# Narrowing a batch search, moving a small copy, and doing the last norm's row work during the gates

## The chip, the cores and the metric

The kernel runs on one core of one Trainium2 chip. The metric is device time in microseconds (us); lower is better. In the profile PE is TensorE, DVE is VectorE, ACT is ScalarE, POOL is GpSimd and SP is the engine that issues the DMAs.

## The reference, cut to what matters

There are 3327 nodes with 128 features each; `adj` is a sparse matrix with entries from 0.05 to 1 and a full diagonal. Everything is float32.

```python
# layer 0, two steps (x_a starts as x; a second branch multiplies by the row-normalized adj)
logits = (Xa @ W1.T @ W2.T) @ (Xa @ W3.T).T
probs = softmax(logits)                       # keep the largest of a row until their sum reaches 0.9
keep_sorted = cumsum(sorted) - sorted < 0.9
A = probs * mask; A = A / A.sum(-1)
Xa = A @ Xa;  Z = Z + Xf @ U1[n].T + Xa @ U2[n].T
x = layernorm(x + layernorm(X + Z) * ln_g + ln_b)
# layer 1: node_support = adj_offdiag @ x; edge_support from three attention heads with vectors a
r = sigmoid(ir + hr); z = sigmoid(iz + hz); n = tanh(inn + r * hn)
gru = (1 - z) * n + z * h                     # twice: "edge" and "node", each with its own weights
out = layernorm(x + diag[:, None] * gru_edge + diag[:, None] * gru_node)
```

## The kernel before, in words

Rows are handled as T = 26 tiles of 128, padded to 3328. The kernel is three stages one behind the other, each with one instruction stream per engine and semaphores between them: `layer0`, `normalize_and_sum` and `attention_and_gates`.

**The batch at the end of layer 0.** Of every row the largest values are found in segments (MAX8, L73) and a threshold is searched by halving an interval of float bit patterns (`solve_halving`): each halving (L222) masks and sums all candidates, compares the sum with 0.9 of the row's total (L227) and moves the middle (L229). In the second step rows whose segments don't cover their threshold are gathered into one batch of up to 128 rows; `taken_batch` searches it with segments of 16, which are 208 x 8 = 1664 candidates a row, in 16 halvings. Behind the halvings come one pass below the last middle (L235), a MAX8 over it (L240), a pass above the value found (L258) and small steps (`end`). The flags go to TensorE (`turn_flags`, L918), which turns them only after its own `late_rows`; then VectorE reads them (L1594) and selects, full width (L451, L456, L462). A flag of 256 or more, from any open row, runs `another_round` over the full width first. Meanwhile ScalarE copies the late rows' results (L1236, L1250, L1255) and GpSimd adds them (L767).

**The first norm.** In `normalize_and_sum` VectorE sums the two halves of the rows, then waits for TensorE's products of the head vectors (L1736) and copies them into V (L1866); then come the deviation (L1832), the root on ScalarE (L1797, after the squares, L1790), and in each half the rows are scaled (L1872) and added to X (L1876). X is shifted before by GpSimd, in two halves (L1725), and L1872 waits for its half. V is read by TensorE's `project`, behind the turned rows.

**The gates and the last norm.** `gates_and_output` works in 14 units: 7 chunks of 512 columns (the last has 256), each once for "edge" (g = 0) and once for "node" (g = 1). TensorE does six products a unit (`products`, L2015 to L2024) into four banks of sums, of two sets. ScalarE does the sigmoids r (L2045), z (L2049) and s (L2051). VectorE does the candidate of unit u (L2076, L2080), then the blend of unit u - 1 (L2087 to L2096). Behind all units, chunk by chunk, TensorE turns the blended columns to rows (L2034), VectorE adds them to H with their sums (L2109, L2113), ScalarE squares (L2056); then the root (L2061), the reciprocal (L2119), and VectorE norms 26 tiles (L2122). SP stores the first 13 tiles, then 12, then the last tile's 127 rows (L1995, L1999, L2002).

The order of all work is written by hand: each engine executes its stream in order.

## Time and profile before

| | us |
|---|---|
| median of 3 runs | 2689.44 (2689.21 to 2690.14) |
| the profiled execution | 2681.91 |
| its span, first to last instruction | 2680.1 |
| PE busy in the span | 2326.0 (87%) |
| DVE busy | 2159.6 (81%) |
| ACT busy | 1070.0 (40%) |
| POOL busy | 149.3 (6%) |

The rows further down are of the profiled execution; their times count from the start of its span. A row of the timeline gives the start, the duration from the first to the last instruction of a group, the engine, the line, the operation, what it writes and reads, and the number of instructions; in brackets stands the idle time before it and what ended it. The mean granted clock of TensorE is 0.95 of its full speed.

### The profile page before, as it was taken

What the parts mean: (1) busy time and instruction counts of PE and PEld (TensorE: products, weight loads), DVE (VectorE), ACT (ScalarE), POOL (GpSimd) and SP (SyncE); (2) the same over time, 40 slices, a digit from 0 to 9 for tenths busy, and PEclk for the clock granted to TensorE, in tenths of its full rate; (3) what the DMA queues carried; (4) which work ended last, traced back from release to release, by engine and by line L of the source; (5) the groups of instructions that cost most, each with busy time, mean ns of one, the idle gap of its engine ahead of it and who ended that gap; (6) DMA issues with size and microseconds to landing.
All of it is one profiled execution on the core that took longest, in us unless ns stands there. A gap on an engine that the chain in (4) does not pass through costs nothing. (4 is left out here: it accounts for less than half of the span.)

```text
span 2680.1 us, 53786 instructions
## 1 busy us (share of the span) xinstructions
PE 2326.0 (87%) x17795; PEld 1967.5 (73%) x17795; DVE 2159.6 (81%) x6687; ACT 1070.0 (40%) x1803; POOL 149.3 (6%) x342
## 2 busy tenths in 40 slices
PE   7999999878899979988976459987999999999995
PEld 2666666657677867767756459876999999999962
DVE  4777777578787888888889677757999999999956
ACT  5666666433334444334422230004344433444333
POOL 0000000111111111000010000000000000000000
PEclk8999999989999989999978769999999999999997
DMA  4000000022223322222212135542343343333320
GB/s 134 2 2 1 1 1 1 2 103 78 81 101 116 116 78 104 103 78 82 105 48 83 63 134 213 206 178 103 105 136 124 120 139 104 131 128 112 121 92 26
DMA packets 57310, 244.88 MB, mean 91 GB/s; under 512 B 6929, under 2 KB 18576, under 8 KB 43344
## 3 DMA queue, kind: packets, MB, share of 16 engines
q1 hardware_dynamic: 57040, 241.99, 25.8%
q8 instruction: 83, 1.36, 0.2%
q14 instruction: 187, 1.53, 0.2%
HBM read 235.15 MB, written 6.82 MB: 90 GB/s over the span
## 5 line engine op out<-in xcount | busy, mean ns | idle before, releaser
L2319 PE MATMUL a_acc<-H,pT 128*128 128x128 f32 x4056 | 547.8, 277 | 11.8 <-ACT a_rows L2352 3.8
L2319 PEld LDWEIGHTS a_acc<-H,pT 128*128 128x128 f32 x4056 | 495.3, 192 | 28.8 <-DVE pT L2455 20.0
L992 PE MATMUL small<-XR,wT 128*128 128x128 f32 x2756 | 379.0, 283 | 26.7 <-ACT wT L1262 26.1
L992 PEld LDWEIGHTS small<-XR,wT 128*128 128x128 f32 x2756 | 344.3, 197 | 42.6 <-ACT wT L1262 42.6
L863 PE MATMUL lg<-kT,qs 128*128 128x512 f32 (+1 forms) x742 | 339.8, 594 | 27.3 <-ACT e L1180 16.8
L73 DVE MAX8 cand<-e 128x8 f32<-128x64 f32 (+3 forms) x1898 | 302.8, 241 | 48.8 <-issue 25.3
L2455 DVE TENSOR_TENSOR pT<-a_tr,a_adjT 128x512 f32<-128x512 f32 (+1 forms) x546 | 316.7, 645 | 20.7 <-PE a_tr L2278 15.6
L2278 PE MATMUL a_tr<-ident,prob 128*128 128x128 f32 x2028 | 311.2, 273 | 10.9 <-ACTq L2346 10.9
L1262 ACT ACTIVATE wT<-tr 128x512 f32<-128x512 f32 (+1 forms) x371 | 206.7, 566 | 276.9 <-PE tr L982 275.9
L892 PE MATMUL accR<-XR,adj 128*128 128x129 f32 x2704 | 312.6, 275 | 0.0
L892 PEld LDWEIGHTS accR<-XR,adj 128*128 128x128 f32 x2704 | 308.5, 192 | 0.0
L2433 DVE CUSTOM_DVE_ANT_0 prob<-a_adj,EB 128x3328 f32<-128x3328 f32 x78 | 282.6, 3623 | 0.0
L982 PE MATMUL tr<-ident,e 128*128 128x128 f32 x1378 | 217.8, 287 | 65.6 <-DVE scalars L1516 60.0
L982 PEld LDWEIGHTS tr<-ident,e 128*128 128x128 f32 x1378 | 169.7, 148 | 117.1 <-DVE scalars L1516 62.8
L863 PEld LDWEIGHTS lg<-kT,qs 128*128 128x128 f32 x742 | 118.7, 193 | 186.5 <-ACT e L1180 142.4
L1180 ACT ACTIVATE e<-lg 128x512 f32<-128x512 f32 (+1 forms) x371 | 206.6, 566 | 107.8 <-PE lg L863 106.0
L2278 PEld LDWEIGHTS a_tr<-ident,prob 128*128 128x128 f32 x2028 | 240.9, 142 | 11.1 <-issue 11.1
L2344 ACT ACTIVATE prob<-prob,a_negmax 128x3328 f32<-128x3328 f32 x78 | 238.9, 3063 | 9.1 <-DVE a_negmax L2442 9.1
L1752 PE MATMUL g_sp<-g_adj,H 128*128 128x128 f32 x1352 | 159.2, 279 | 17.1 <-ACTq L1817 17.1
L1752 PEld LDWEIGHTS g_sp<-g_adj,H 128*128 128x128 f32 x1352 | 155.1, 194 | 18.8 <-issue 18.8
L1212 ACT ACTIVATE e<-e,scalars 128x3327 f32<-128x3327 f32 x53 | 162.0, 3059 | 8.4 <-DVE scalars L1580 8.3
L222 DVE SCALAR_TENSOR_TENSOR work<-cand,mid 128x416 f32<-128x416 f32 (+1 forms) x198 | 143.3, 758 | 10.6 <-issue 3.1
(351 smaller groups left out, 2419.8 us busy)
## 6 DMA issues: line engine op xcount, KB each, us to landing
adj<-in_adjT SPq DMA_DIRECT2D x52, 1664.0 KB, 7.2
g_adj<-in_adjT SPq DMA_DIRECT2D x26, 1664.0 KB, 6.8
a_adj<-in_adj SPq DMA_DIRECT2D x26, 1664.0 KB, 7.0
a_adjT<-in_adjT SPq DMA_DIRECT2D x156, 256.0 KB, 3.9
a_adjT<-in_adjT SPq DMA_DIRECT2D x26, 128.0 KB, 4.1
XT<-in_x_t SPq DMA_DIRECT2D x1, 1664.0 KB, 7.2
hT_scratch<-hT SPq DMA_DIRECT2D x1, 1664.0 KB, 11.3
nsT_scratch<-nsT SPq DMA_DIRECT2D x1, 1664.0 KB, 5.3
```

The costliest lines, as they stand in the source:

```text
L73: eng.max(cand[:, n, :], src[:, n * seg:min((n + 1) * seg, width)])
L863: eng.matmul(lg[bank(st, p, k, c)][:, 0:sl.stop - sl.start], qs[k][:, :], kT[:, sl], start=True, stop=True).then_inc(lg_ready, 1)
L892: mm = eng.matmul(accR[:, :], adj[k][:, j * P:(j + 1) * P], xf[:, j, :], start=False, stop=(j == T - 1))
L982: mm = eng.transpose(tr[(k * NC + c) % 2][:, o:o + P], e[b][k][:, j * P:(j + 1) * P], ident[:, :])
L992: mm = eng.matmul(accA[:, :], wT[(k * NC + c - 1) % 2][:, o:o + P], xa[:, j, 0:P], start=(j == 0), stop=(j == T - 1))
L1262: eng.activation(wT[(k * NC + c) % 2][:, 0:sl.stop - sl.start], tr[(k * NC + c) % 2][:, 0:sl.stop - sl.start], ACT.Copy).then_inc(wT_ready, 1)
L1752: mm = eng.matmul(sp[k][:, :], H[:, j, :], adj[q][:, j * P:(j + 1) * P], start=(j == 0), stop=(j == T - 1))
L2278: mm = eng.transpose(tr[g % BANKS][:, (j % 4) * P:(j % 4 + 1) * P], prob[order[n][1]][:, j * P:(j + 1) * P], ident[:, :])
L2319: mm = eng.matmul(acc[:, :], pT[g % RING][:, (j % 4) * P:(j % 4 + 1) * P], H[:, j, :], start=(j == 0), stop=(j == T - 1))
L2344: eng.activation(prob[h][:, :], prob[h][:, :], ACT.Exp, bias=negmax[h][:, :], accum_out=den[h][:, :])
L2433: eng.tensor_tensor_reduce(prob[h][:, :], adj[k][:, :], EB[:, h, :], 1.0, -3.0e38, ALU.add, ALU.max, mx[h][:, :])
L2455: eng.tensor_tensor(pT[g % RING][:, 0:width(c)], tr[g % BANKS][:, 0:width(c)], adjT[:, c * 512:c * 512 + width(c)], ALU.mult).then_inc(pT_ ...
```

## The change

It has three parts.

**Batch search.** `solve_halving` takes an argument `wide`. For the batch it is 6: after six halvings `narrow` masks the candidates that are not below the current bound, keeps the largest 8 of each 64 (26 groups, 208 values) and one more value, the largest sum so far that stayed below 0.9; the largest eighth value of a group raises `tau`, the bound above which all values are known to be among the candidates. The other ten halvings and the steps behind them run over these 209 values.

**Head vectors.** The wait for the head vectors' products and the three copies into V stand behind the second mean of the two halves.

**Gates and last norm.** Each set has three banks; z has one bank for both sets, and the turned rows have one. TensorE turns chunk c behind unit 2c + 3, VectorE adds its rows behind blend 2c + 3, at unit 2c + 4, and ScalarE squares them behind unit 2c + 5. The last two chunks come behind all units. VectorE norms 14 tiles, ScalarE 12, from a new product of mean and reciprocal; five stores instead of three.

```diff
+WIDE_HALVINGS = 6
...
         self.counts = sb("counts", [P, 2, 4])
-        self.round_cand = sb("round_cand", [P, -(-width // ROUND_SEG), 8])
+        n_round = -(-width // ROUND_SEG)
+        self.few_cand = sb("few_cand", [P, n_round * 8 + 1])
+        self.round_cand = self.few_cand[:, 0:n_round * 8].rearrange("p (a b) -> p a b", b=8)
...
-    def solve_halving(self, eng, cand, halvings):
+    def narrow(self, eng, cand, step, done):
+
+        mass, low = self.mass[:, 0:done, 0:1], self.low[:, 0:done, 0:1]
+        spare, rest = self.work[:, 0:cand.shape[1]], self.few_cand.shape[1] - 1
+        eng.tensor_tensor(low, mass, self.one("theta", 0).unsqueeze(1).to_broadcast([P, done, 1]), ALU.is_lt)
+        eng.tensor_scalar(self.round_mid[:, :], self.mid[:, 0:1], float(step), None, ALU.add)
+        eng.drain()
+        eng.scalar_tensor_tensor(spare, cand, self.round_mid[:, :].bitcast(F32), cand, ALU.is_lt, ALU.mult)
+        eng.tensor_tensor(low, mass, low, ALU.mult)
+        eng.drain()
+        segment_tops(eng, spare, cand.shape[1], self.round_cand, cand.shape[1] * 8 // rest)
+        eng.tensor_reduce(self.few_cand[:, rest:rest + 1], low.rearrange("p n k -> p k n"), AX.X, ALU.max)
+        eng.drain()
+        eng.tensor_reduce(self.one("best", 0), self.round_cand[:, :, 7], AX.X, ALU.max)
+        eng.drain()
+        eng.tensor_tensor(self.one("tau", 0), self.one("tau", 0), self.one("best", 0), ALU.max)
+        eng.drain()
+
+    def solve_halving(self, eng, cand, halvings, wide=None):
 
 
         tiles, n = range(len(cand)), len(cand)
...
         eng.drain()
         step = FIRST_STEP
         for h in range(halvings):
+            if h == wide:
+                self.narrow(eng, cand[0], step, h)
+                cand = [self.few_cand[:, :]]
+                spare = [self.work[:, 0:cand[0].shape[1]]]
             for k in tiles:
                 eng.scalar_tensor_tensor(spare[k], cand[k], self.mid[:, k:k + 1].bitcast(F32), cand[k],
                                          ALU.is_ge, ALU.mult, accum_out=self.mass[:, h, k:k + 1])
...
-                        find.solve_halving(eng, [find.fine[:, :, :].rearrange("p a b -> p (a b)")], FINE_HALVINGS)
+                        find.solve_halving(eng, [find.fine[:, :, :].rearrange("p a b -> p (a b)")], FINE_HALVINGS,
+                                           wide=WIDE_HALVINGS)
...
                     eng.tensor_reduce(total[:, half(i)], H[:, half(i), :], AX.X, ALU.add)
                     eng.drain()
                     mean(half(i))
-                eng.wait_ge(v_summed, 1)
-                for part in range(3):
-                    copy = eng.tensor_copy(V[:, part, :], vp[:, :, part % 2])
-                copy.then_inc(v_ready, 1)
                 for i in range(2):
                     deviation(0, i)
                     eng.wait_ge(x_shifted, i + 1)
...
                                                  ALU.mult, ALU.add, accum_out=total[:, t:t + 1])
                     eng.drain()
                     mean(half(i))
+                eng.wait_ge(v_summed, 1)
+                for part in range(3):
+                    copy = eng.tensor_copy(V[:, part, :], vp[:, :, part % 2])
+                copy.then_inc(v_ready, 1)
                 clear_diagonal(0, 0)
                 for i in range(2):
                     deviation(1, i)
...
     edge = sb(3, "o_edge", [P, CH])
-    sums = [banks[0:4], [banks[4], banks[7], banks[5], banks[6]]]
+    sums = [banks[0:3], banks[3:6]]
+    zp_bank, rows_bank = banks[6:8]
 
...
+    BY_VECTOR = T // 2 + 1
+    PARTS = [(0, BY_VECTOR // 2), (BY_VECTOR // 2, BY_VECTOR), (BY_VECTOR, (BY_VECTOR + T) // 2),
+             ((BY_VECTOR + T) // 2, T)]
 
     def tiles(c):
         return range(c * 4, min(c * 4 + 4, T))
 
-    def rows_bank(c):
-        return sums[c // 4][c % 4]
+    def rows_of(t):
+        return rows_bank[:, (t % 4) * P:(t % 4 + 1) * P]
 
         eng.dma_start(support[1][:, cols(NC - 1)], d["gsT"][:, cols(NC - 1)]).then_inc(chunk_loaded[NC - 1], 16)
-        eng.wait_ge(normed, 1)
-        eng.dma_start(d["out"][0:HALF * P, :].rearrange("(t p) d -> p t d", p=P), H[:, 0:HALF, :])\
-           .then_inc(stored, 16)
-        eng.wait_ge(normed, 2)
         whole = N // P
-        eng.dma_start(d["out"][HALF * P:whole * P, :].rearrange("(t p) d -> p t d", p=P), H[:, HALF:whole, :])\
-           .then_inc(stored, 16)
+        for n in (0, 2, 1, 3):
+            first, end = PARTS[n][0], min(PARTS[n][1], whole)
+            eng.wait_ge(normed[n // 2], n % 2 + 1)
+            eng.dma_start(d["out"][first * P:end * P, :].rearrange("(t p) d -> p t d", p=P), H[:, first:end, :])\
+               .then_inc(stored, 16)
         if N % P:
             eng.dma_start(d["out"][whole * P:N, :], H[0:N % P, whole, :]).then_inc(stored, 16)
-        eng.wait_ge(stored, 48 if N % P else 32)
+        eng.wait_ge(stored, 80 if N % P else 64)
 
     def products(eng):
+        def turn(c):
+            eng.wait_ge(mixed, 2 * c + 2)
+            eng.wait_ge(mean_ready, c) if c else eng.wait_ge(sup_copied, T)
+            for t in tiles(c):
+                mm = eng.transpose(rows_of(t), OT[:, t * P:(t + 1) * P], ident[:, :])
+            mm.then_inc(turned, 1)
+
         eng.wait_ge(weights, 16 * 8)
         for u in range(UNITS):
             c, g, i = u // 2, u % 2, u % 2
-            rp, zp, inp, hnp = (t[:, 0:width(c)] for t in sums[i])
+            rp, inp, hnp, zp = (t[:, 0:width(c)] for t in sums[i] + [zp_bank])
             if g == 0:
                 eng.wait_ge(chunk_loaded[c], 48)
             if u >= 2:
...
             eng.matmul(rp, Wh[g][:, 0:P], state, start=True, stop=False)
             eng.matmul(rp, Wi[g][:, 0:P], sup, start=False, stop=True).then_inc(r_summed, 1)
             eng.matmul(inp, Wi[g][:, 2 * P:3 * P], sup, start=True, stop=True).then_inc(in_summed, 1)
-            if u >= 2:
-                eng.wait_ge(z_ready, u - 1)
-            if u == 1:
-                eng.wait_ge(sup_copied, T)
+            if u >= 1:
+                eng.wait_ge(z_ready, u)
             eng.matmul(zp, Wh[g][:, P:2 * P], state, start=True, stop=False)
             eng.matmul(zp, Wi[g][:, P:2 * P], sup, start=False, stop=True).then_inc(z_summed, 1)
-        for c in range(NC):
-            if c == 0:
-                eng.wait_ge(arg_ready, UNITS - 1)
-                eng.wait_ge(z_ready, UNITS - 1)
-            if c == 4:
-                eng.wait_ge(arg_ready, UNITS)
-                eng.wait_ge(z_ready, UNITS)
-            eng.wait_ge(mixed, 2 * c + 2)
+            if u >= 3 and u % 2:
+                turn((u - 3) // 2)
+        turn(NC - 1)
+
+    def gates(eng):
+        def squares(c):
+            eng.wait_ge(mean_ready, c + 1)
             for t in tiles(c):
-                mm = eng.transpose(rows_bank(c)[:, (t % 4) * P:(t % 4 + 1) * P], OT[:, t * P:(t + 1) * P],
-                                   ident[:, :])
-            mm.then_inc(turned, 1)
-
-    def gates(eng):
+                eng.activation(sq[:, t, :], H[:, t, :], ACT.Square, bias=negmean[:, t:t + 1],
+                               accum_out=var[:, t:t + 1])
+            eng.drain()
+            eng.sem_inc(squared, 1)
+
         eng.wait_ge(biases_ready, 1)
         for u in range(UNITS):
             c, g, i = u // 2, u % 2, u % 2
             n = width(c)
-            rp, zp, inp, hnp = sums[i]
+            rp, inp, hnp = sums[i]
+            zp = zp_bank
             eng.wait_ge(r_summed, u + 1)
             eng.activation(r[i][:, 0:n], rp[:, 0:n], ACT.Sigmoid, bias=b_rz[g][:, 0:1]).then_inc(r_ready, 1)
             eng.wait_ge(z_summed, u + 1)
...
             eng.wait_ge(arg_ready, u + 1)
             eng.activation(s[i][:, 0:n], arg[i][:, 0:n], ACT.Sigmoid, scale=2.0, bias=b_new[g][:, :])\
                .then_inc(s_ready, 1)
-        for c in range(NC):
-            eng.wait_ge(mean_ready, c + 1)
-            for t in tiles(c):
-                eng.activation(sq[:, t, :], H[:, t, :], ACT.Square, bias=negmean[:, t:t + 1],
-                               accum_out=var[:, t:t + 1])
-            eng.drain()
-            eng.sem_inc(squared, 1)
+            if u >= 5 and u % 2:
+                squares((u - 5) // 2)
+        squares(NC - 2)
+        squares(NC - 1)
         eng.wait_ge(var_ready, 1)
         eng.activation(var[:, :], var[:, :], ACT.Sqrt).then_inc(std_ready, 1)
+        eng.wait_ge(rstd_ready, 1)
+        for first, end in PARTS[2:]:
+            for t in range(first, end):
+                eng.activation(H[:, t, :], H[:, t, :], ACT.Identity, bias=shift[:, t:t + 1],
+                               scale=rstd[:, t:t + 1])
+            eng.drain()
+            eng.sem_inc(normed[1], 1)
 
     def blends(eng):
         eng.wait_ge(weights, 16 * 8)
...
             eng.drain()
             eng.sem_inc(mixed, 1)
 
+        def rows(c):
+            own = slice(tiles(c)[0], tiles(c)[-1] + 1)
+            eng.wait_ge(turned, c + 1)
+            for t in tiles(c):
+                eng.scalar_tensor_tensor(H[:, t, :], rows_of(t), diag[:, t:t + 1], H[:, t, :],
+                                         ALU.mult, ALU.add, accum_out=total[:, t:t + 1])
+            eng.drain()
+            eng.tensor_scalar(negmean[:, own], total[:, own], -1.0 / P, None, ALU.mult)
+            eng.drain()
+            eng.sem_inc(mean_ready, 1)
+
         candidate(0)
         for u in range(1, UNITS):
             candidate(u)
             blend(u - 1)
+            if u >= 4 and u % 2 == 0:
+                rows((u - 4) // 2)
         blend(UNITS - 1)
-        for c in range(NC):
-            own = slice(tiles(c)[0], tiles(c)[-1] + 1)
-            eng.wait_ge(turned, c + 1)
-            for t in tiles(c):
-                eng.scalar_tensor_tensor(H[:, t, :], rows_bank(c)[:, (t % 4) * P:(t % 4 + 1) * P],
-                                         diag[:, t:t + 1], H[:, t, :], ALU.mult, ALU.add,
-                                         accum_out=total[:, t:t + 1])
-            eng.drain()
-            eng.tensor_scalar(negmean[:, own], total[:, own], -1.0 / P, None, ALU.mult)
-            eng.drain()
-            eng.sem_inc(mean_ready, 1)
+        rows(NC - 2)
+        rows(NC - 1)
         eng.wait_ge(squared, NC)
         eng.tensor_scalar(var[:, :], var[:, :], 1.0 / P, EPS, ALU.mult, ALU.add).then_inc(var_ready, 1)
         eng.wait_ge(std_ready, 1)
         eng.reciprocal(rstd[:, :], var[:, :])
         eng.drain()
-        for t in range(T):
-            eng.tensor_scalar(H[:, t, :], H[:, t, :], negmean[:, t:t + 1], rstd[:, t:t + 1],
-                              ALU.add, ALU.mult)
-            if t in (HALF - 1, T - 1):
-                eng.drain()
-                eng.sem_inc(normed, 1)
+        eng.tensor_tensor(shift[:, :], negmean[:, :], rstd[:, :], ALU.mult)
+        eng.drain()
+        eng.sem_inc(rstd_ready, 1)
+        for first, end in PARTS[:2]:
+            for t in range(first, end):
+                eng.tensor_scalar(H[:, t, :], H[:, t, :], negmean[:, t:t + 1], rstd[:, t:t + 1],
+                                  ALU.add, ALU.mult)
+            eng.drain()
+            eng.sem_inc(normed[0], 1)
 
     return early_loads, late_load_and_stores, products, gates, blends
```

## Rows read from the trace of the kernel before

**Rows 1.** Timeline, batch search, VectorE: start us, us, engine, line, operation, tiles.

```profile
1457.62 1.95 DVE L222 SCALAR_TENSOR_TENSOR work<-cand,mid 128x1664 f32<-128x1664 f32 x1
...
1484.03 0.17 DVE L233 TENSOR_TENSOR low<-mass,scalars 128x16 f32<-128x16 f32 x1
...
1486.23 1.89 DVE L240 MAX8 sorted<-work 128x8 f32<-128x1664 f32 x1
...
1490.05 1.95 DVE L258 SCALAR_TENSOR_TENSOR work<-cand,scalars 128x1664 f32<-128x1664 f32 x1
```

**Rows 2.** One line's instructions (ns min/median/max), and two timeline rows of VectorE.

```profile
L222 DVE SCALAR_TENSOR_TENSOR work<-cand,mid x198: 646/651/1953, 553.0 to 1481.5; 128x416 f32<-128x416 f32 x182, 128x1664 f32<-128x1664 f32 x16
...
970.08 6.68 DVE L73 MAX8 cand<-e 128x8 f32<-128x64 f32 x52
...
1507.03 3.68 DVE L462 SCALAR_TENSOR_TENSOR e<-work,scalars,e 128x3328 f32<-128x3328 f32 x1
```

**Rows 3.** The timeline of ScalarE, GpSimd and TensorE at the search's end.

```profile
1490.39 0.38 ACT L1255 ACTIVATE XT<-xz 128x256 f32<-128x256 f32 x1 [0.80 <-PE xz L911]
1490.85 1.73 POOL L767 TENSOR_TENSOR H<-H,XT 128x256 f32<-128x256 f32 x1 [1.38 <-ACT XT L1255]
...
1496.98 0.08 PEld L918 LDWEIGHTS small<-ident,pair_flags 128*1 128x1 f32 x1 [6.83 <-issue]
```

**Rows 4.** First norm: two timeline rows, then two lines' instructions.

```profile
1538.71 1.28 ACT L1797 ACT_TABLE_LOAD   x1
...
1541.63 0.30 DVE L1866 COPY V<-g_vp 128x3 f32<-128x3 f32 x3 [5.94 <-PE g_vp L1736]
...
L1725 POOL TENSOR_TENSOR ln_x<-ln_x,ln_bias x2: 3690/3693/3696, 1539.4 to 1543.3; 128x1664 f32<-128x1664 f32 x2
...
L1872 DVE SCALAR_TENSOR_TENSOR H<-H,ln_negmean,ln_gain x26: 339/343/3395, 1543.7 to 1558.3; 128x128 f32<-128x128 f32 x26
```

**Rows 5.** Gates, busy us: PE, PEld, DVE, ACT, POOL; clock, DMA share, GB/s.

```profile
2577.40:2644.50 67.10, 67.10 (x171) 31.99 (x171) 45.47 (x67) 27.30 (x42) 0.00 (x0) 1.00 0.01 3
```

**Rows 6.** The timeline of ScalarE, VectorE and TensorE in the gates.

```profile
2631.74 0.69 ACT L2045 ACTIVATE prob<-a_tr,EB 128x512 f32<-128x512 f32 x1 [1.28 <-PE a_tr L2017]
2632.46 0.75 DVE L2076 SCALAR_TENSOR_TENSOR prob<-a_tr,EB,prob 128x512 f32<-128x512 f32 x1 [1.50 <-ACT prob L2045]
...
2637.61 0.75 DVE L2076 SCALAR_TENSOR_TENSOR prob<-a_acc,EB,prob 128x512 f32<-128x512 f32 x1 [0.73 <-ACT prob L2045]
...
2644.44 2.65 PE L2034 MATMUL a_tr<-ident,EB 128*128 128x128 f32 x20
```

**Rows 7.** Timeline of the last norm: ScalarE, VectorE, store queue.

```profile
2576.36 0.28 ACT L2361 ACTIVATE a_rowsT<-a_small 128x128 f32<-128x128 f32 x1 [0.42 <-PE a_small L2291]
...
2649.96 0.35 DVE L2109 SCALAR_TENSOR_TENSOR H<-a_tr,diag,H 128x128 f32<-128x128 f32 x1
...
2651.50 0.35 DVE L2109 SCALAR_TENSOR_TENSOR H<-a_tr,diag,H 128x128 f32<-128x128 f32 x1
...
2651.84 0.39 ACT L2056 ACTIVATE EB<-H,EB 128x128 f32<-128x128 f32 x1
...
2662.87 0.18 DVE L2117 TENSOR_SCALAR EB<-EB 128x26 f32<-128x26 f32 x1 [2.80 <-ACTq L2058]
...
2664.84 6.97 DVE L2122 TENSOR_SCALAR H<-H,EB 128x128 f32<-128x128 f32 x26
...
2668.32 0.39 SPq L1995 DMA_DIRECT2D out_rows<-H  x1
```

**Rows 8.** Busy time by stretch while the output is stored.

```profile
2669.00:2670.00 1.00, 0.00 (x0) 0.00 (x0) 1.00 (x5) 0.00 (x0) 0.00 (x0) 0.50 0.73 211
...
2673.00:2674.00 1.00, 0.00 (x0) 0.00 (x0) 0.00 (x0) 0.00 (x0) 0.00 (x0) 0.50 1.04 291
...
2675.00:2676.00 1.00, 0.00 (x0) 0.00 (x0) 0.00 (x0) 0.00 (x0) 0.00 (x0) 0.50 0.58 155
...
2677.00:2678.00 1.00, 0.00 (x0) 0.00 (x0) 0.00 (x0) 0.00 (x0) 0.00 (x0) 0.50 0.07 21
```

More of the change, by code:

```diff
@@ L1947, in gates_and_output @@
     total, negmean = sb(0, "o_total", [P, T]), sb(0, "o_negmean", [P, T])
-    var, rstd = sb(0, "o_var", [P, T]), sb(0, "o_rstd", [P, T])
-    sums = [banks[0:4], [banks[4], banks[7], banks[5], banks[6]]]
+    var, rstd, shift = sb(0, "o_var", [P, T]), sb(0, "o_rstd", [P, T]), sb(0, "o_shift", [P, T])
+    sums = [banks[0:3], banks[3:6]]
+    zp_bank, rows_bank = banks[6:8]
     weights = sem("o_weights")
@@ L1958, in gates_and_output @@
     turned, mean_ready, squared = sem("o_turned"), sem("o_mean_ready"), sem("o_squared")
-    var_ready, std_ready = sem("o_var_ready"), sem("o_std_ready")
-    normed, stored = sem("o_normed"), sem("o_stored")
-    HALF = T // 2
+    var_ready, std_ready, rstd_ready = sem("o_var_ready"), sem("o_std_ready"), sem("o_rstd_ready")
+    normed = [sem("o_normed_vector"), sem("o_normed_scalar")]
+    stored = sem("o_stored")
+    BY_VECTOR = T // 2 + 1
+    PARTS = [(0, BY_VECTOR // 2), (BY_VECTOR // 2, BY_VECTOR), (BY_VECTOR, (BY_VECTOR + T) // 2),
+             ((BY_VECTOR + T) // 2, T)]
     def width(c):
@@ L2073, in candidate @@
             n = width(c)
-            rp, zp, inp, hnp = sums[i]
+            rp, inp, hnp = sums[i]
             eng.wait_ge(r_ready, u + 1)
```

## The prediction

> **What bounds the kernel now.** I read the stretches of the three edits in the timeline and, for the end of the kernel, busy time by stretch. The page puts TensorE at 87% of the span and VectorE at 81%, but the edits lie where one of them waits for the other, so each is read from its own stretch.
>
> The batch search: VectorE halves over 1664 candidates, 2.64 us a halving (ten of them from 1457.62 to 1484.03), then a tail of small steps and three wide ones [rows 1]. TensorE meanwhile does late rows. Their last result is copied out by ScalarE at 1490.39 + 0.38 = 1490.77, and TensorE's next instruction, the turned flags, starts only at 1496.98, because it waits for the search [rows 3]. So the search has 6.2 us on the path; what it saves beyond that is free time.
>
> The norm: VectorE copies the head vectors at 1541.63 after 5.94 us of idling for TensorE's products, and only then goes on to the deviations [rows 4].
>
> The end: during the gates TensorE is busy 67.10 of 67.10 us at full granted clock, VectorE 45.47, ScalarE 27.30; 12 whole units and two half ones are 5.15 us a unit [rows 5]. So the gates are bound by TensorE's products. Behind them only 26 transposes are left to TensorE, and the last 35 us are a chain of VectorE, ScalarE and stores.
>
> **The batch search.** The first six halvings stay. In place of ten wide ones come the narrowing and ten narrow ones. Width 416 took 0.65 us and 1664 took 1.95 [rows 2], 1.04 ns an element, so 209 elements take an estimated 0.43, and a halving 2.64 - 1.52 = 1.12 us; ten, 11.2. The narrowing: one wide pass with its product step, 2.1; 26 tops of 64 elements at 6.68 / 52 = 0.128 [rows 2], 3.3; its four other drained steps at about 0.25 each, 1.0; together 6.4. Change so far 26.4 - 17.6 = 8.8 us. In the tail the two wide passes (1.95) and the wide MAX8 (1.89) [rows 1] lose about 1.5 each: 4.5. The flags come 13.3 us earlier, at about 1483.6, and TensorE is now the late one: the flags are turned at 1490.85 instead of 1496.98, **a gain of 6.1 us**. It stays 6.1 unless the narrowing costs over 7 us more than I think. What could take some back is GpSimd's last add, at 1490.85 [rows 3], now beside the first selecting steps: it took 1.73 there while a wide VectorE pass was running; with VectorE waiting it should end before the mark steps begin, 1.3 us after the flags. Bounds 5.2 to 6.2. The selection, the products after it and the placing are the same and shift as a block.
>
> Whether the narrowing leaves a row open depends on the data: a row fails if in one of the 26 groups at least 8 candidates lie over its cut and below the sixth halving's bound. Worked out from the reference's formulas and inputs: 38 rows reach the batch because a 64-wide segment didn't cover their cut; in the fullest group of any of them there are 5 such candidates. So no further round.
>
> **The head vectors.** Without the wait the first deviation step runs at 1538.7, when the squares are done, and the root after the table load of 1.28 us ends at about 1540.2 [rows 4]. But the next step waits for x shifted by GpSimd, whose first half, from 1539.4, ends at 1543.1; before, it began at 1543.7. That is at most 0.5 us early. And there GpSimd's second half starts, at 1543.3: of the 26 vector steps of this line one took 3395 ns against 343 [rows 4], it stood until GpSimd was through at 1547.0. Starting earlier only lengthens that stand, except for at most one step of 0.27 that may slip in first. The three copies (0.30) now lie behind the second mean, where VectorE is what the squares, the root and the turned rows wait for. Nothing hides them: **+0.2 us**, between -0.2 and +0.3. The products that read V come only behind the last turned rows and don't wait for them.
>
> The Trainium skill ("SBUF — State Buffer", section "Who interferes with whom") says that a vector instruction with two inputs in SBUF and a GpSimd one that reads SBUF exclude each other for their whole length, whoever issues first. By it the edit gives nothing; by the vector queue's own times it would give 0.5. The row of 3395 ns agrees with the Trainium skill.
>
> **The gates and the last norm.** Three things change.
>
> (a) On TensorE the 24 transposes of six chunks move in behind every second unit. 20 of them took 2.65 us with 0.11 from start to start [rows 6], so a chunk costs 0.45; five of these lie ahead of unit 12, and its start moves from 2639.26 to about 2641.5. A pair of units becomes 10.30 + 0.45 = 10.75 us long.
>
> (b) On VectorE each pair had idle times of 1.50 and 0.73 us [rows 6]. A chunk of rows is 1.54 us from first to first [rows 7]: it follows the long blend (idle 0.73), so the odd unit's candidate is about 0.85 late, and the 1.50 absorbs that. On ScalarE four squares (0.39 each and a readout) are 1.65 us between an odd unit's last sigmoid and the next unit's first. The loop through both is: first sigmoid to candidate 0.7, candidate, blend and rows 6.0, next candidate 1.5, sigmoid 0.7, squares 1.75, in all 10.65 us against TensorE's 10.75. So I let TensorE stay the bound, with nearly no slack. The single z bank is read 0.7 us after it is written, and its next product comes 3.4 us into the next unit: no wait. The rows' bank must be read before the next chunk's turn: 0.8 us to spare.
>
> (c) The end. Unit 11's products end at 2641.05; ScalarE has its last two sigmoids until 2642.5 and four squares until 2644.15, and only then, 1.1 us late, unit 12's first. So the candidate of 12 begins at 2644.6, blend 11 ends at 2648.7, rows of chunk 4 at 2650.2, candidate 13 at 2651.1, blends 12 and 13 at 2652.6 and 2654.65. Then come two chunks of rows in place of seven: 2656.2; the last transposes wait for the shared bank, 0.6; the last two tiles with mean and drains 0.95: 2657.75. Squares end at 2658.65 against 2662.87. From there to the norming it was 2.0 us, with the table load [rows 7], plus 0.25 for the shift: 2660.9. The norming began at 2664.84 before: 3.9 gained.
>
> VectorE now norms 14 tiles and ScalarE 12. VectorE's step is 6.97 / 26 = 0.27 us, so its first 7 are stored from 2662.8 (before: 13, from 2668.32 [rows 7]), and it ends at 2664.7. ScalarE's norming has no row; a square of the same size with readout is 0.39, which makes 12 tiles 4.7 us, and below it I take the 0.28 of a copy of that size [rows 7]: 3.4 to 4.7, that is 2664.4 to 2665.7. Either way the stores are the bound: they ran at about 290 GB/s, beginning 0.95 us after the first issue (share 0.73 of the us from 2669) [rows 8], and the 1.64 MB of whole tiles need 5.65 us. So data flow from 2663.8 to 2669.45. Before, the flow ended at 2675.6 and the span 4.5 later, of which some 3 us are the last 127 rows at about 20 GB/s, on one engine's share of 0.07 [rows 8]; I leave that as it is. End at 2673.9 against 2680.1: **a gain of 6.2 us**. The two stores more are hidden behind the flow. Bounds: 2.5 (the loop in b 0.6 us longer than TensorE's pair, in five chunks, and ScalarE's norming slow) to 7.5 (unit 12's delay on ScalarE absent and the flow a little faster).
>
> No row shows ScalarE's Identity after a root. The Trainium skill ("ScalarE: Activation LUTs", section "Table sets: the hidden batching unit") says that cheap functions, identity among them, are in every set, so no load; if it were wrong, 1.28 us would stand before ScalarE's tiles, of which the flow hides all but a few tenths.
>
> **Sum.** -6.1 + 0.2 - 6.2 = -12.1 us. The profiled execution took 2681.91 (span 2680.1), the sum makes it 2669.8. The median of the runs is 2689.44, 7.5 above the profiled one; the difference is carried over whole: **2677.3 us**.
>
> **Rivals.**
> 1. The loop of (b) binds. For it: 0.1 us of slack is less than what I can read; two new waits cross between the engines in every pair. Against it: only five chunks, and the loop reaches the end once. At 0.6 a chunk it costs 3: 2680.3.
> 2. The late rows hide less: the narrowing or GpSimd's add takes 1 to 2 us of the search's gain, or the head copies cost their whole 0.3. 2678.5. Against it: 7 us of cover.
> 3. The end goes better: ScalarE's squares don't delay unit 12's first sigmoid, and five smaller stores start flowing sooner, up to 3 us. 2674.5.
> 4. The wait for the head vectors was on the path, so its removal gives 0.5 more: 2676.8. The stand of 3395 ns speaks against it. By the rule of the Trainium skill above it can't be.
> 5. Slower: a batch row stays open, and a whole further round runs in the selection. Its price: three full-width steps of 3.7 us [rows 2], 26 wider tops 5, ten halvings of about 1.4, a tail of 7, together some 37 us; less the gain, +25: 2714. It decides from 8 candidates in a group; the count says 5.
>
> **How the numbers follow.** The forecast has 0.60, rival 1 has 0.14, rival 2 0.07, rival 3 0.10, rival 4 0.03, rival 5 0.02; 0.04 is left for a stall that I don't see, in the gates most likely, which eats all of the gain. The likeliest case's own range is 2675 to 2680. With rivals 1 and 3 in, and the bounds of (c), it is 2673 to 2682. A measurement tells 0.2% from no change, 5.4 us, so under 2684.1 is faster. Forecast and rivals 1 to 4 are all under it, but with two of them together and the open stall I leave 0.07 for no difference, and 0.04 for slower: 0.89 faster.
>
> **What would show it.** In the changed profile: ten narrow halvings about 1.1 us apart and the flags turned right behind ScalarE's last copy of late rows, not behind VectorE; no wait before the first deviation, but one vector step of over 3 us still there; TensorE still at some 10.75 us a pair without idling longer than 0.3 between units; first store about 5.5 us earlier, and the span ending 11 us after the first store's issue. Wrong: full-width steps beyond three in the batch's selection; TensorE waiting in the gates for VectorE's means or for z; a table load before ScalarE's norming.

## The result and the profile after

The changed kernel takes 2674.69 us (median of 7 runs, 2672.60 to 2680.83), the kernel before on the same chip 2688.88 (7 runs, 2683.28 to 2690.14). The ratio is 0.9956, 95% interval 0.9945 to 0.9967, that is 8.9 to 14.8 us less. It is worked out from all runs and is not the ratio of the two medians, which lie 14.2 us apart; the same holds for the ratios further down. The forecast was 2677.3 us, faster, from 2673 to 2682.

The profiled execution of the changed kernel took 2674.69 (span 2672.9), that of before 2681.91, less than any of the 7 runs of before in this comparison. The two traces are therefore only 7.2 us apart. Split into stretches, each from the end of the one above it, in us:

| stretch | before | after | difference |
|---|---|---|---|
| start to the last search's first halving | 1441.87 | 1442.82 | +0.95 |
| to the flags turned | 55.11 | 51.19 | -3.92 |
| to the first norm's sums | 34.33 | 34.15 | -0.18 |
| to its third scaling step (L1884; after, L1910) | 33.19 | 32.96 | -0.23 |
| to the first gate product | 1012.96 | 1014.40 | +1.44 |
| to the end | 102.64 | 97.38 | -5.26 |

The rows of 0.95 and 1.44 contain no edit; the others add up to -9.6. No experiment below edits the attention (the fifth stretch) either, and over all 14 traces it scattered from 1012.9 to 1019.0 us; most of what single traces differ by outside the edited stretches is there. So I read the parts from stretches, and the whole from the comparisons of many runs.

The search, after, VectorE; then ScalarE, TensorE and GpSimd where the flags are turned (to set beside [rows 1] and [rows 3]):

```profile
1458.87 1.95 DVE L210 SCALAR_TENSOR_TENSOR work<-cand,round_mid 128x1664 f32<-128x1664 f32 x1
1460.97 3.40 DVE L74 MAX8 few_cand<-work 128x8 f32<-128x64 f32 x26
1465.00 0.44 DVE L247 SCALAR_TENSOR_TENSOR work<-few_cand,mid 128x209 f32<-128x209 f32 x1
...
1475.98 0.18 DVE L258 TENSOR_TENSOR low<-mass,scalars 128x16 f32<-128x16 f32 x1
1476.67 0.37 DVE L265 MAX8 sorted<-work 128x8 f32<-128x209 f32 x1
1483.75 0.16 DVE L1616 TENSOR_TENSOR pair_flags<-pair_flags,scalars 128x1 f32<-128x1 f32 x1
```

```profile
1493.58 0.38 ACT L1280 ACTIVATE XT<-xz 128x256 f32<-128x256 f32 x1 [0.80 <-PE xz L936]
1494.01 0.08 PEld L943 LDWEIGHTS small<-ident,pair_flags 128*1 128x1 f32 x1 [0.66 <-ACT XT L1280]
1494.04 0.72 POOL L792 TENSOR_TENSOR H<-H,XT 128x256 f32<-128x256 f32 x1 [1.37 <-ACT XT L1280]
1494.32 0.28 DVE L1620 TENSOR_REDUCE pair_flag_int<-small 1x1 int32<-1x128 f32 x1 [10.42 <-PE small L943]
```

VectorE has its flags at 1483.91, 41.09 us after the first halving (before, 55.01), and then idles 10.42 us. What releases the flags is now the late rows' last copy. No further round ran: from the turned flags to the norm's sums it takes as long as before.

The first norm, after (beside [rows 4]):

```profile
1535.57 1.28 ACT L1823 ACT_TABLE_LOAD   x1
1535.96 3.70 POOL L1751 TENSOR_TENSOR ln_x<-ln_x,ln_bias 128x1664 f32<-128x1664 f32 x1 [41.20 <-DMA ln_gain<-in_ln_g]
1539.75 6.94 DVE L1894 SCALAR_TENSOR_TENSOR H<-H,ln_negmean,ln_gain 128x128 f32<-128x128 f32 x13 [2.40 <-POOLq L1753]
1539.84 3.81 POOL L1751 TENSOR_TENSOR ln_x<-ln_x,ln_bias 128x1664 f32<-128x1664 f32 x1 [0.18 <-issue]
```

The wait for the products is gone; a wait of 2.40 us for GpSimd's first half stands in its place, and the 13 steps take 6.94 us, since one of them stands until GpSimd's second half is through. The bracket of the first GpSimd row says what GpSimd itself waited for: the load of `ln_gain`.

The gates, after: one window (columns as in [rows 5]), TensorE's turns of a chunk, VectorE's candidates, ScalarE's first sigmoid of unit 12:

```profile
2575.50:2644.80 69.30, 69.30 (x190) 33.70 (x188) 49.84 (x102) 33.56 (x74) 0.00 (x0) 1.00 0.01 4
```

```profile
2617.60 0.60 PE L2039 MATMUL a_small<-ident,EB 128*128 128x128 f32 x4
2628.34 0.60 PE L2039 MATMUL a_small<-ident,EB 128*128 128x128 f32 x4
...
2621.54 0.75 DVE L2114 SCALAR_TENSOR_TENSOR prob<-a_tr,EB,prob 128x512 f32<-128x512 f32 x1 [1.00 <-ACT prob L2079]
...
2627.62 0.75 DVE L2114 SCALAR_TENSOR_TENSOR prob<-a_tr,EB,prob 128x512 f32<-128x512 f32 x1
...
2642.27 0.47 ACT L2079 ACTIVATE prob<-a_tr,EB 128x256 f32<-128x256 f32 x1
```

TensorE is busy the whole window; from turn to turn it is 10.74 us. The odd unit's candidate (2627.62) follows the added rows with no idle time, the even one's (2621.54) still has 1.00.

The end, after (beside [rows 7] and [rows 8]); the windows' columns are those of [rows 5]:

```profile
2654.83 0.66 PE L2039 MATMUL a_small<-ident,EB 128*128 128x128 f32 x2 [5.36 <-DVEq L2146]
2655.53 0.35 DVE L2142 SCALAR_TENSOR_TENSOR H<-a_small,diag,H 128x128 f32<-128x128 f32 x1 [0.87 <-PE a_small L2039]
2657.40 0.18 DVE L2159 TENSOR_SCALAR EB<-EB 128x26 f32<-128x26 f32 x1 [0.99 <-ACTq L2069]
2657.43 1.28 ACT L2092 ACT_TABLE_LOAD   x1
2659.62 4.93 ACT L2096 ACTIVATE H<-H,EB 128x128 f32<-128x128 f32 x12 [0.67 <-DVEq L2164]
2659.68 3.89 DVE L2168 TENSOR_SCALAR H<-H,EB 128x128 f32<-128x128 f32 x14
2661.62 3.53 SPq L2028 DMA_DIRECT2D out_rows<-H  x4
2665.20 1.29 SPq L2031 DMA_DIRECT2D out_rows<-H  x1
```

```profile
2663.00:2664.00 1.00, 0.00 (x0) 0.00 (x0) 0.57 (x3) 1.00 (x4) 0.00 (x0) 0.50 0.99 284
...
2668.00:2669.00 1.00, 0.00 (x0) 0.00 (x0) 0.00 (x0) 0.00 (x0) 0.00 (x0) 0.50 0.35 93
...
2670.00:2671.00 1.00, 0.00 (x0) 0.00 (x0) 0.00 (x0) 0.00 (x0) 0.00 (x0) 0.50 0.07 22
```

### The profile page after: what moved, and what is told of

The parts are those of the page before. It is cut to its first block and busy times, and to the rows that moved or that the text cites. A ratio compares the mean times of both kernels' runs of the same rounds, so it can differ in the third digit from the quotient of the medians.

```text
span 2672.9 us, 53835 instructions
## 1 busy us (share of the span) xinstructions
PE 2330.9 (87%) x17795; PEld 1971.5 (74%) x17795; DVE 2141.0 (80%) x6709; ACT 1074.3 (40%) x1815; POOL 148.4 (6%) x342
## 5 line engine op out<-in xcount | busy, mean ns | idle before, releaser
L247 DVE SCALAR_TENSOR_TENSOR work<-cand,mid 128x416 f32<-128x416 f32 (+1 forms) x188 | 123.7, 694 | 9.9 <-issue 3.1
```

## The experiments

### The three parts, one at a time, and the whole again

Each kernel is the one before with one part of the change: the search; the copies into V; `gates_and_output`. The fourth is the changed kernel itself.

> The kernel before with the narrowed batch search alone. My theory (the late rows on TensorE bound the gain): VectorE has the flags some 13 us after the sixth wide halving's end earlier than before, but they are turned right behind ScalarE's last copy of late rows, and the whole kernel gains 4 to 6 us. Rival (the search itself was the bound): the flags are turned as soon as VectorE has them and the gain is about 13 us. Rival (a batch row stays open): full-width steps beyond three in the batch's selection and about 37 us lost.

> The kernel before with the head vectors' copies moved alone. My theory (the shift on GpSimd bounds this place): the wait of 5.9 us before the first deviation is gone, one wait for GpSimd's first half takes its place, and the time from the norm's first sum to the third scaling changes by less than 0.4 us; the whole kernel is the same within its noise. Rival (the wait was on the path): 3 to 5.9 us gained in that stretch.

> The kernel before with the gates' and the last norm's change alone. My theory: from the first gate product to the end of the span it takes 97 to 98 us in place of 102.6, since TensorE's unit pairs take 10.75 us without idling between units and the stores then flow at one piece; 5 us gained. Rival (the loop through rows and squares binds): pairs of over 11 us, TensorE idle behind the z product or the turn, gain under 3 us.

> The changed kernel again, unchanged, in the same rounds as its three parts. My theory (three independent stretches): its gain is the sum of the three parts' gains within the noise, 10 to 14 us. Rival (the parts share a resource or a phase of TensorE's clock): the sum differs from the whole by more than 4 us.

Measured, against 2689.65 for the kernel before (29 runs on the same chip):

| | median us | ratio (95%) | edited stretch, us, from its trace |
|---|---|---|---|
| search alone | 2679.68 | 0.9975 (0.9964 to 0.9986) | 55.11 to 48.77 |
| copies alone | 2686.91 | 0.9996 (0.9986 to 1.0007) | 33.19 to 32.93 |
| gates and norm alone | 2683.46 | 0.9982 (0.9970 to 0.9994) | 102.64 to 97.97 |
| all three | 2674.85 | 0.9951 (0.9937 to 0.9966) | 51.01; 33.07; 97.47 |

The ratios' losses add up: 0.25 + 0.04 + 0.18 = 0.47% against 0.49% for all three, 12.6 us against 13.2. Each has an interval of some 3 to 4 us to either side, so this excludes only a large hindrance between the parts. The copies can't be told from nothing.

With the search alone the flags are turned 6.3 us sooner after its start; in the two traces of the whole change only 3.9 and 4.1. The late rows tell why: they end 48.7 us after the search's start with the search alone and 51.1 and 51.0 with the whole change, and the difference is in their first products. TensorE, after:

```profile
1446.92 7.50 PE L917 MATMUL accR<-XR,adj 128*128 128x129 f32 x52
1455.27 5.97 PE L917 MATMUL accR<-XR,adj 128*128 128x129 f32 x52
...
1445.00:1450.00 5.00, 4.53 (x22) 4.53 (x22) 4.61 (x8) 0.77 (x2) 0.73 (x1) 0.50 0.02 3
1450.00:1455.00 5.00, 4.45 (x40) 4.29 (x39) 4.54 (x11) 0.37 (x1) 0.00 (x0) 0.99 0.00 0
```

The search alone:

```profile
1444.73 5.97 PE L917 MATMUL accR<-XR,adj 128*128 128x129 f32 x52
1451.55 5.97 PE L917 MATMUL accR<-XR,adj 128*128 128x129 f32 x52
...
1440.00:1445.00 5.00, 4.02 (x23) 3.52 (x23) 4.55 (x15) 1.05 (x3) 0.00 (x0) 0.69 0.00 0
1445.00:1450.00 5.00, 5.00 (x48) 5.00 (x47) 4.54 (x11) 0.09 (x1) 1.48 (x1) 1.00 0.01 3
```

TensorE had idled some 12 us before both, and was granted half of its speed (1.2 of 2.4 GHz). Worked out from the mean clocks of these windows, it was back at full speed at about 1443.1 in the second trace and at about 1450.1 in the first. Its first product after the idle time was at 1439.6 and 1440.9, so the return came 3.4 us behind it in one and 9.2 in the other. The change alone doesn't decide which: of the traces with the narrowed search and all late rows ahead of the flags, the search alone, the split tail and the norm on VectorE (the last two below) end the late rows after 48.7 to 49.0 us, the changed kernel, its repeat and four more (ten wide halvings, 10 tiles on ScalarE, and the two without GpSimd's shift) after 50.9 to 51.3; with the old search, before and the copies alone took 48.9, the gates alone 50.8. What sets the return stays open. While the search bound, the 2 us were hidden; now they count.

### How much cover the search has

`WIDE_HALVINGS = 10`: four narrow halvings made wide again.

> The changed kernel with ten wide halvings ahead of the narrowing in place of six (VectorE's search about 6.1 us longer). My theory (late rows on TensorE hide it): VectorE has the flags 47 us after the first wide halving in place of 41, and the flags are turned 49 to 51 us after it as before, behind ScalarE's last copy; nothing lost. Rival (the search's end is still on the path): the turn comes 6 us later too.

One run, 2675.55 us. VectorE has its flags 46.76 us after the search's start, 5.7 later than in the changed kernel; they are turned at 51.19, the same to 0.01. So what four of the ten narrow halvings save buys nothing: the search's gain is capped by the late rows (46.76 lies below the 48.7 us of their early end too).

### Turning the flags between two late rows

```diff
-rows(LATE[2][0], 1)
+rows_of(LATE[2][0], 1, 0)
+turn_flags(PAIRS)
+rows_of(LATE[2][0], 1, 1)
 ...
-turn_flags(PAIRS)                # behind late_rows()
```

> The changed kernel with the batch's flags turned between the two halves of the last late rows, not behind all of them. My theory: the flags are there about 41 us after the first wide halving, the turn comes at 41 to 42 us in place of 49 to 51, VectorE's selection (about 14 us) then runs beside TensorE's last rows, and the stretch from the first wide halving to the norm's first sum shrinks by 7 to 9 us. Rival (something else, such as GpSimd's adds or TensorE's clock behind the selection, holds the batch): under 4 us.

2670.93 us, ratio 0.9934 (0.9913 to 0.9954). From its trace, TensorE, VectorE, GpSimd and ScalarE:

```profile
1483.22 0.08 PEld L943 LDWEIGHTS small<-ident,pair_flags 128*1 128x1 f32 x1 [3.90 <-DVEq L1618]
1483.62 7.61 PE L917 MATMUL accR<-XR,adj 128*128 128x129 f32 x52
...
1493.12 3.69 DVE L487 SCALAR_TENSOR_TENSOR e<-work,scalars,e 128x3328 f32<-128x3328 f32 x1
1493.58 3.81 POOL L792 TENSOR_TENSOR H<-H,XT 128x256 f32<-128x256 f32 x1 [18.88 <-ACT XT L1281]
1497.53 0.38 ACT L1281 ACTIVATE XT<-xz 128x256 f32<-128x256 f32 x1 [3.12 <-POOLq L793]
1497.97 1.57 PEld L1007 LDWEIGHTS tr<-ident,e 128*128 128x128 f32 x8 [2.87 <-ACT XT L1281]
```

Now TensorE waits 3.90 us for VectorE, and the last late chunk lies beside the selection. Search start to the norm's sums takes 76.2 us against 82.9 to 85.5 in the traces with the changed code there, 6.7 to 9.3 less. This trace is of those with the early return of the clock; against the three others of that kind (82.9 to 83.4) it is 6.7 to 7.2. The medians (against the 2674.85 above) show only 3.9, with an interval 11 us wide.

GpSimd's add, 0.72 us when alone, stands 3.81 beside VectorE's full-width step, and through ScalarE's copy it holds TensorE, but not for long: VectorE's last small step before TensorE's next product (the reciprocal) ends at 1497.64, 0.3 us before that product; another small step of VectorE, 0.52 us in place of 0.16, stood some 0.4 beside the add. The kernel with both improvements (last below) shows the same: there VectorE releases this product, the first late product behind the flags runs at full clock (5.97 us in place of the 7.61 above, during which the granted clock fell to half), and the late rows end 4.1 us sooner after the search's start; yet search start to the norm's sums takes 76.1 us. So the bound is VectorE's selection again, and the scatter of the late rows is hidden again.

### The end of the kernel

The last store is of 127 rows. Split, it is 112 and 15:

```diff
-eng.dma_start(d["out"][whole * P:N, :], H[0:N % P, whole, :])
+even = N % P // 16 * 16
+eng.dma_start(d["out"][whole * P:whole * P + even, :], H[0:even, whole, :])
+eng.dma_start(d["out"][whole * P + even:N, :], H[even:N % P, whole, :])
 ...
```

> The changed kernel with the last tile's 127 rows stored as 112 and 15. My theory (127 rows go through one DMA engine, at about 20 GB/s for 3 us): the span ends 8.5 us behind the first store in place of 11.3, 2.5 to 3 us gained at the end. Rival (the end is the fixed completion time of the last store): no gain, or 0.4 lost by one more issue.

2671.81 us, ratio 0.9939 (0.9919 to 0.9959); gates to end 94.18 us against 97.38 and 97.47. Windows of this kernel:

```profile
2663.00:2664.00 1.00, 0.00 (x0) 0.00 (x0) 0.00 (x0) 0.00 (x0) 0.00 (x0) 0.50 0.99 260
2664.00:2665.00 1.00, 0.00 (x0) 0.00 (x0) 0.00 (x0) 0.00 (x0) 0.00 (x0) 0.50 0.15 40
```

The flow stops at once; the 3 us and more at a share of 0.07 are gone and the span ends 3.2 us sooner, although SP issues one store more. From the first store's issue to the end it is 8.1 us in place of 11.3. The Trainium skill ("DMA: Bandwidth & Descriptors", section "Why a DMA increments its semaphore by 16 and not by 1") says that a transfer goes over the largest number of engines up to 16 that divides the slowest dimension of both its sides, one for 127 rows. The share of 0.07, one in 16, and this run agree.

Next, all 26 tiles normed by VectorE in two halves, as before the change, and the rest as after (`PARTS = [(0, T // 2), (T // 2, T)]`):

> The changed kernel with all 26 tiles of the last norm on VectorE and three stores, as before the change; rows and squares stay among the gates. My theory: the first store then comes 1.6 us later (13 tiles in place of 7) and the span ends 2 to 3 us later than in the changed kernel, so of the 5.3 us gained from the first gate product to the end about 3 are the rows' and 2.3 the divided norming's. Rival (the stores' flow hides the division): the same end within 0.5 us.

One run, 2672.72 us; gates to end 99.43, 2.0 more than the changed kernel. Of the 5.3 us that the last part gains, the divided norming (with its five stores) is 2.0, and moving the rows into the gates the other 3.2.

Last, ScalarE is given 10 tiles, VectorE 16 (`BY_VECTOR = T // 2 + 3`):

> The changed kernel with 16 tiles of the last norm on VectorE and 10 on ScalarE in place of 14 and 12 (0.28 us a tile on VectorE, 0.41 on ScalarE). My theory (the stores' flow at about 290 GB/s is the bound from its first byte): the norming ends 0.3 to 0.5 us earlier, the first store comes 0.3 later since its part has 8 tiles, and the span's end moves with the first store, 0 to 0.3 us later. Rival (the slower engine's last tile sets the end): 0.4 us earlier.

One run, 2677.38 us (its attention stretch is the longest of all, 1019.0); gates to end 97.71, 0.3 more. Its two engines now end within 0.3 us of each other (2666.05 and 2666.35), and it helps nothing: the first store waits for 8 tiles instead of 7 and comes 0.25 later. So the stores' flow and its start are the bound, as far as one trace tells.

### What holds the first norm

GpSimd's shift of X is left out (ln_b isn't added); in the second kernel the copies into V are also back at their place before the first deviation.

> The changed kernel without GpSimd's shift of x in the first norm (the bias ln_b is left out of the result). My theory (the shift sets when the first scaling starts and blocks VectorE's two-input steps): the first scaling starts about 9 us after the norm's first sum in place of 11.6, no step of it stands over 3 us, and the third scaling starts 27 to 28 us after the first sum in place of 33. Rival (the scaling is bound by the roots and squares on ScalarE): under 1 us.

> The same without GpSimd's shift (ln_b left out), and with the head vectors' copies back at their old place, ahead of the first deviation. My theory (only the shift hides what the copies' move is worth): without the shift the old place costs 2.5 to 4 us against the new one in the stretch from the norm's first sum to the third scaling. Rival (the copies' wait was free in any case): the two are within 0.4 us.

2671.77 and 2672.22 us, one run each. The norm's sums to the third scaling step take 27.19 and 30.12 us (changed kernel 32.96). The first of the two, VectorE:

```profile
1537.77 0.24 DVE L1857 RECIPROCAL ln_rstd<-ln_var 128x13 f32<-128x13 f32 x1 [1.40 <-ACT ln_var L1820]
1538.09 3.50 DVE L1891 SCALAR_TENSOR_TENSOR H<-H,ln_negmean,ln_gain 128x128 f32<-128x128 f32 x13
```

No wait before the scaling and no long step in it: GpSimd's shift holds this norm for 5.8 us, 2.4 as a wait and 3.4 as the stand. And with the shift gone the place of the copies is worth 2.9 us. Both figures are from one trace each. So the wait that was moved is real; in the kernel as it is, another one ends later.

The other traces agree, and they tell what the move costs. GpSimd starts its shift 7.7 to 8.6 us behind the norm's first sum. Counted from that start, the third scaling step comes 25.08 to 25.10 us later in the three traces without the move (before, the search alone, the gates alone) and 25.13 to 25.16 in the nine with it. So the stretch scatters with GpSimd's start, and the move costs 0.05 us. In every one of them the profile names the landing of the load of `ln_gain` as what releases GpSimd; in the changed kernel SP issues this load 4.35 us behind the first sum (1532.51), after an issue for `ln_bias` that takes 3.82. No run here moves these loads ahead.

### Both improvements

The flags turned early and the store split:

> The changed kernel with the flags turned between the last late rows' halves and the last tile stored as 112 and 15 rows. My theory (two independent stretches): from the first wide halving to the norm's first sum 76 to 77 us in place of 84 to 85, from the first gate product to the end 94.2 in place of 97.4; 9 to 12 us faster than the changed kernel, 21 to 25 faster than the one before, near 2664. Rival (one of the two gains is eaten by the spread of the stretches between): under 6 us against the changed kernel.

2664.86 us (2661.70 to 2670.85) against 2690.62, ratio 0.9915 (0.9889 to 0.9942): faster than both kernels. All four runs lie below all 13 of the changed kernel, though these were taken in other comparisons. In its trace the search to the norm's sums takes 76.08 and gates to end 94.22; the two gains, 6.8 to 9.4 and 3.2 us, stand beside each other.

## Why the prediction was right

**The search.** Narrowing 6.44 us (predicted 6.4), ten halvings 10.98 (11.2), flags 13.9 us earlier at VectorE (13.3), and the turned flags released by ScalarE, not by VectorE: right in each step. The gain of 6.1 is 6.3 where the late rows ran as in the trace of before, and 3.9 in the profiled run of the changed kernel. What the prediction lacked is that these rows themselves scatter by 2 us, with TensorE's clock, which the old search hid. It is the size of rival 2, by a cause that rival 2 doesn't name. GpSimd's add took 0.72 us, not 1.73, as the waiting VectorE let it.

**The head vectors.** Predicted +0.2 us, between -0.2 and +0.3. The stretch took 32.95 to 33.29 us in three traces without the move; with it 32.86 to 33.08 in seven, 33.35 and 33.78 in two. With the scatter of GpSimd's start taken off, the cost is 0.05 us: the predicted sign, a quarter of the size. The mechanism holds: the stand is there, 3.4 us longer than a usual step, and rival 4, which expected 0.5 gained, is out. In the changed trace one scaling step slips in ahead of GpSimd's second half, the 0.27 that the prediction allowed and did not take.

**The gates.** The pair of units 10.74 us (10.75). The changed trace enters the gates 1.94 us sooner; that added back, unit 12's first sigmoid is at 2644.21 (predicted 2644.15) and its candidate at 2644.72 (2644.6). Rival 1, the loop, didn't bind: TensorE is busy 69.30 of 69.30. Rival 3 is out too: unit 12's first sigmoid comes right behind the four squares, and the stores flow from about 1 us after the first issue (0.95 predicted).

**The end.** From there small pieces came late, on the same footing: the last rows are done 0.7 later than predicted. Of this 0.5 is there before chunk 5's rows begin, nearly all of it in the last blend, whose steps have idle times of 0.19 and 0.43 us for which the profile names no releaser; and some 0.2 is the last pair of transposes, 0.66 us for two at half the full clock, where four took 0.60 earlier at full clock. With the 1.94 added back, norming begins at 2661.62 (predicted 2660.9), the first store is issued at 2663.56 (2662.8), 4.8 us earlier than before and not 5.5, and the end is at 2674.84 (2673.9). The gain is 5.3 instead of 6.2. ScalarE's norming took 4.93 us for 12 tiles, above the bounds of 3.4 to 4.7: from tile to tile it is 0.385, as for a square, and the rest is the drain between its two parts and the last tile's own 0.48. It cost nothing that shows, since its last tiles are stored last and the flow took some 5.7 us, as predicted (5.65). No table load stands before it.

**The whole.** The parts, 6.1 - 0.2 + 6.2 = 12.1 us, measured 13.2 (9.1 to 17) and 11.8 (8.9 to 14.8). The forecast of 2677.3 was 2.6 too high. Of that 0.6 is that the kernel before was 0.6 lower in the new comparison (2688.88); the other 2.0 lie inside the interval of 8.9 to 14.8. By the edited stretches of the two profiled runs the gain is only 9.6; it would be 12.0 with the 6.3 that the search gave where the late rows end early, in place of 3.9. So it is in part luck that the whole came out so near to 12.1: the search's term was too large by up to 2.2 us and the end's by 0.9, and the intervals are too wide to show it. Carrying the profiled run's distance from its median over whole did no harm only because the sum was made as a difference: before ran 7.0 us under its median when profiled, the changed kernel exactly at it. The attention's scatter is the likely reason (before's stretch, 1012.96, is the second shortest of the 14), but it isn't shown, since the other runs left no trace.

## What to carry to other kernels

- Speed up a search only until the other engine is the late one; then move the hand-over (here the turned flags, three lines) into that engine's stream. That took 6.7 us or more off the stretch, while making four of the narrow halvings wide again had cost nothing.
- Before removing a wait, look for the next one behind it, and take that away in a test kernel: the new place of the copies cost 0.05 us, and was worth 2.9 with another engine's shift gone.
- Look at the DMA share in the last microseconds of a kernel. At one engine's share, the row count of the store is the first thing to try.

## What the runs showed of the hardware

- A GpSimd add of 128x256 is 0.72 us alone and 3.81 beside a VectorE step with two full-width inputs that was issued 0.46 us before it; the reverse, VectorE's scaling step of 0.35 us, took 3.78 beside GpSimd's add of 128x1664. In these rows whichever came second stood until the other was through.
- TensorE's return from half to full granted clock, after some 12 us of idling at the same place of kernels whose code is the same up to there, came 3.4 us behind its first product in one trace and 9.2 in another (estimated from the mean granted clock of windows of 5 us), and moved the work behind it by 2 us. Whether it differs between executions of one program or between programs, one or two traces of each can't tell.
- ScalarE's norming step with a scale and a bias for each row comes every 0.385 us for a tile of 128x128, as often as a square of that size with its sum; between the two parts, with a drain, it is 0.58.
- A store of 127 rows of 512 bytes ran at some 20 GB/s at a DMA share of 0.07, that of one engine in 16; as 112 and 15 rows it ended 3.2 us sooner.
